# Macaron block (feed-forward, S4 convolution, feed-forward) on one core: first tile reordered, shared low-rank product of A's upper half, PdT copied ahead

## The reference

```
x = x + 0.5 * ffn(layernorm(x))
x = x + s4(layernorm(x))            # causal convolution with a kernel K of length 512, plus D * u
x = x + 0.5 * ffn(layernorm(x))

def qlinear(x, q, scale, A, B):     # 4-bit weights and a low-rank part of rank 32
    w = (q - 7.5) * (scale * 0.005)[:, None]
    return x @ w.T + 0.02 * (x @ A @ B)
def ffn(x):
    h = silu(qlinear(x, gate)) * qlinear(x, up)     # 512 -> 1376
    return qlinear(h, down)                         # 1376 -> 512
```

## Time and profile before

| | |
|---|---|
| median of 3 runs | 589.48 us |
| profiled execution, whole | 588.72 us |
| its span | 586.7 us |
| PE busy | 566.7 us, 97% of the span |
| PE weight loads | 436.4 us, 74% |
| DVE busy | 403.0 us, 69% |
| ACT busy | 303.2 us, 52% |
| POOL busy | 229.5 us, 39% |
| mean granted PE clock | 0.993 of full |

### The profile page before, as it was taken

How to read it: one execution, slowest core, us unless ns; L and a number is a source line. 1 busy time by engine, 2 the same in 40 slices (tenths; PEclk the granted TensorE clock), 3 DMA queues, 4 the chain that set the end, 5 groups by cost and what they waited for, 6 DMA issues and landing times.

```text
span 586.7 us, 12166 instructions
## 1 busy us (share of the span) xinstructions
PE 566.7 (97%) x4656; PEld 436.4 (74%) x4656; DVE 403.0 (69%) x766; ACT 303.2 (52%) x748; POOL 229.5 (39%) x248
## 2 busy tenths in 40 slices
PE   6799998999989999999999999999999999999996
PEld 6544675436678887888778887788877888788975
DVE  6577864886489867599576995479844888455544
ACT  5476412666238851478505784158831676236621
POOL 5446500030205980059701596026850367105510
PEclk9899998999999999999999999999999999999999
DMA  8983302003323074001820019000190202540001
GB/s 287 374 272 120 72 11 69 13 0 64 73 15 14 12 112 86 10 1 20 146 44 10 2 20 177 13 11 1 26 178 11 77 1 43 94 149 5 1 2 73
DMA packets 87266, 39.75 MB, mean 68 GB/s; under 512 B 75849, under 2 KB 80713, under 8 KB 87209
## 3 DMA queue, kind: packets, MB, share of 16 engines
q1 hardware_dynamic: 86393, 38.84, 29.5%
q10 hardware_dynamic: 816, 0.14, 0.1%
HBM read 16.42 MB, written 4.19 MB: 35 GB/s over the span
## 4 chain that ended last, share of the span: by engine, by line
PE 91%; DVE 4%; ACT 2%; issue 1%; DVEq 1%; DMA 1%; ACTq 0%
PE banks L1436 35%; PE banks L1359 28%; PE banks L1419 11%; PE banks L1401 5%; PE banks L1565 4%; PE banks L1324 3%; PE banks L1378 2%; PE banks L1395 1%; ACT p_stack L638 1%; DVEq L858 1%; DMA X<-in_x 1%; PE banks L1554 1%; DVE stats L857 1%; PE banks L1585 0%; DVE zs L869 0%
## 5 line engine op out<-in xcount | busy, mean ns | idle before, releaser
L1436 PE MATMUL banks<-xT,w 128*128 128x256 f16 (+1 forms) x1848 | 223.1, 273 | 1.3 <-DVE ring L996 1.3
L1436 PEld LDWEIGHTS banks<-xT,w 128*128 128x128 f16 (+1 forms) x1848 | 182.0, 100 | 22.7 <-issue 1.8
L1359 PE MATMUL banks<-dw,hT 128*128 128x256 f16 (+3 forms) x1408 | 184.8, 286 | 0.0
L1359 PEld LDWEIGHTS banks<-dw,hT 128*128 128x128 f16 (+1 forms) x1408 | 135.7, 98 | 35.0 <-issue 0.9
L955 DVE SCALAR_TENSOR_TENSOR work<-banks,work 128x512 f32<-128x512 f32 (+1 forms) x88 | 60.6, 689 | 59.3 <-PE banks L1401 25.5
L483 POOL TENSOR_TENSOR rstd<-veps,minus_half 128x1 f32<-128x1 f32 x32 | 19.9, 623 | 182.3 <-DVE veps L861 182.1
L1419 PE MATMUL banks<-xT,w 128*128 128x512 f16 (+1 forms) x336 | 80.0, 382 | 1.6 <-DVE work L955 0.7
L554 POOL TENSOR_TENSOR hT<-work,hT 128x512 f16<-128x512 f32 x60 | 70.8, 1181 | 5.0
L551 POOL TENSOR_SCALAR hT<-work 128x512 f16<-128x512 f32 x60 | 37.8, 630 | 89.1 <-DVE work L955 89.1
L1419 PEld LDWEIGHTS banks<-xT,w 128*128 128x128 f16 (+1 forms) x336 | 33.4, 101 | 42.3 <-ACT work L687 2.6
L638 ACT ACTIVATE p_stack<-banks 128x64 f16<-128x64 f32 x96 | 14.6, 226 | 88.2 <-PE banks L1324 83.5
(11 more groups left out here) (176 smaller groups left out, 704.0 us busy)
## 6 DMA issues: line engine op xcount, KB each, us to landing
out_x<-X SPq DMA_DIRECT2D x16, 256.0 KB, 2.6
X<-in_x SPq DMA_DIRECT2D x1, 2048.0 KB, 8.5
ring<-in_gate_q_t SPq DMA_DIRECT2D x2, 768.0 KB, 12.4
hT<-in_up_q_t SPq DMA_DIRECT2D x2, 768.0 KB, 13.1
work<-in_b SPq DMA_DIRECT2D x2, 688.0 KB, 8.8
X<-in_x SPq DMA_DIRECT2D x4, 256.0 KB, 5.1
X<-in_x SPq DMA_DIRECT2D x1, 1024.0 KB, 13.3
ring<-in_down_q_t SPq DMA_DIRECT2D x1, 1024.0 KB, 11.7
```

The lines of the kernel that those rows point to most:

```text
L1359: last = mm(acc(j)[:, 1 - c, 0:width], hT[0:rows[m], m, a, j * P:(j + 1) * P], dw[0:rows[m], m, src], start=(m == 0 and a == 0), stop=(m = ...
L1436: last = mm(dst[0:r, 0:HH], w[:, blocks + k, cols], xT[:, a, 2 * op + k, :], start=(first and k == 0 and a == 0), stop=(k == 1 and a == 1) ...
```

## The change

It has four parts.

1. The first tile is reordered. `warm` is 96 and 28 products instead of 60 and 12. `p_product(0, 1)` and `first_products` are placed earlier; the transposes of P for sub-tiles 1 to 3 later; block 1 of the up product is made between them. ACT makes the high parts of sub-tiles 2 and 3 instead of DVE; DVE copies the transposed sub-tile 1 instead of ACT. The B matrices arrive in two parts of 256 and 1120 columns (the second after chunk 1); ACT scales the first, POOL the second, after its cast of chunk 1. In DVE's blocks of tile 0, `ln_stats(1, .)`, `down_b` and `ln_apply(1, .)` move to later blocks, `down_a` to block 9, with the weight sums behind it in blocks 9 and 10. The Vc-B product moves from the passes into block 9, into bank 4. `s4_b_copy` and `s4_vectors` stand right behind `s4_inverse`, and PE waits for `s4_b_copy` in front of `down_pass(0, 1, 0, EARLY)` instead of in front of tile 1.
2. In fast tiles `p_product` for i = 0 and 2 makes B11 with A's upper half into columns 0-127 of its bank and B21 with the lower half beside it. For i = 1 and 3 it makes T1 and B22 only (8 instructions instead of 12). DVE copies the B11 part out once for each pair and adds it to each half's own part (`p_sum`) into a buffer in SBUF, from which `p_high` and `p_split` now read.
3. ACT's `pd_copy` of j = 1 and 3 stands in front of `p_high` of the same number.
4. `p_high` of fast tiles waits for `p_sum` instead of for `p_product`.

The diff, cut to the core:

```diff
-        b_raw = view(work, 0, P, 2, I)
+        b_raw = X[:, 2 * TS:SUBS, :].rearrange("p s h -> p (s h)")[:, 0:2 * I].rearrange("p (g i) -> p g i", g=2)
+        b_parts = (slice(0, B_FIRST), slice(B_FIRST, I))
...
             cast_gate(0)
+            cast_gate(1)
             for g, wb in enumerate((gb_w, ub_w)):
...
+                if n < FAST:
+                    act.wait_ge(f.p_mm, n * TS + i + 1)
+                else:
+                    act.wait_ge(f.p_sum, (n - FAST) * TS + i + 1)
...
+                pd_copy(n, 1)
                 if more:
                     p_high(n + 1, 1)
-                pd_copy(n, 1)
...
                 pd_high(n, 3)
+                pd_copy(n, 3)
                 if more:
                     p_high(n + 1, 3)
-                pd_copy(n, 3)
...
+            def p_sum(n, i):
+                dve.wait_ge(f.p_mm, n * TS + i + 1)
+                after(dve, f.p_hi, n * TS + i)
+                own = slice(4 * R * (1 + i % 2), 4 * R * (2 + i % 2))
+                if i % 2 == 0:
+                    V.tensor_copy(p_b11, p_bank(n, i)[:, 0:4 * R]).then_inc(f.p_b11, 1)
+                    dve.wait_ge(f.p_b11, ((n - FAST) * TS + i) // 2 + 1)
+                V.tensor_tensor(p32, p_bank(n, i)[:, own], p_b11, ALU.add).then_inc(f.p_sum, 1)
...
-                        if m in (0, 1):
-                            ln_stats(1, 2 * m, 2 * m + 1)
-                        if m == 2:
+                        if m in (2, 3):
+                            ln_stats(1, 2 * m - 4, 2 * m - 3)
+                        if m == 4:
                             down_b()
-                        if m == 4:
+                        if m in (5, 6, 7, 8):
+                            ln_apply(1, m - 5)
+                        if m == 9:
                             down_a()
-                        if m in (3, 5, 6, 7):
-                            ln_apply(1, (3, 5, 6, 7).index(m))
-                        if m in (8, 9):
-                            weight_sum(m - 8, 0, 1)
+                            weight_sum(0, 0, 1)
+                        if m == 10:
+                            weight_sum(1, 0, 1)
...
                 if n == 0:
                     s4_inverse()
+                    s4_b_copy()
+                    s4_vectors()
...
+                elif i % 2 == 0:
+                    sums(0, half(B11, 0))
+                    last = sums(1, half(B21, 2))
                 else:
+                    last = sums(2, half(T1, 0) + half(B22, 2))
...
                 down_pass(n, 0, 1, EARLY)
+                if n == 0:
+                    pe.wait_ge(s_bread, 1)
                 down_pass(n, 1, 0, EARLY)
...
-            warm(60)
+            warm(96)
             x_transpose(0, 0, 2)
-            warm(12)
+            warm(28)
             x_transpose(1, 1, 3)
             pe.wait_ge(s_aw, 1)
             p_product(0, 0)
+            p_product(0, 1)
             first_products(0)
             x_transpose(2, 2, 2)
-            p_product(0, 1)
+            first_products(1)
             x_transpose(3, 3, 3)
-            first_products(1)
...
```

More of the change, by code:

```diff
@@ L30 @@
 CHUNKS = [(0, 2), (2, 5), (5, 8), (8, 11)]
+B_FIRST = 2 * P
 def s4_macaron(nc, x_d, state_d, step_d, gq_d, uq_d, dq_d, scales_d, ds_d, a_d, b_d, da_d, db_d,
@@ L223, in s4_macaron @@
         s_lr = sem("low_rank_a_loaded")
-        s_lrb = [sem(f"low_rank_b_{g}_loaded") for g in ("gate", "up")]
+        s_lrb = [[sem(f"low_rank_b_{g}_part{c}_loaded") for g in ("gate", "up")] for c in range(2)]
         s_lrd = sem("low_rank_down_loaded")
@@ L568, in _ @@
             cast_gate(0)
+            cast_gate(1)
             for g, wb in enumerate((gb_w, ub_w)):
-                pool.wait_ge(s_lrb[g], 16)
-                pool.tensor_scalar(wb[:, :], b_raw[:, g, :], B_SCALE, 0.0, ALU.mult, ALU.add).then_inc(s_bhi[g], 1)
-            for c in range(1, len(CHUNKS)):
+                pool.wait_ge(s_lrb[1][g], 16)
+                pool.tensor_scalar(wb[:, b_parts[1]], b_raw[:, g, b_parts[1]], B_SCALE, 0.0, ALU.mult, ALU.add)\
+                    .then_inc(s_bhi[g], 1)
+            for c in range(2, len(CHUNKS)):
                 cast_gate(c)
@@ L737, in plain_blocks @@
                         h_high(n, m - 1)
-                    if n == 0 and m in (0, 2, 4):
+                    if n == 0 and m == 0:
+                        p_out(2)
+                        p_out(3)
+                    if n == 0 and m in (2, 4):
                         cast_up(1 + m // 2)
@@ L1068, in tile @@
                     s4_inverse()
+                    s4_b_copy()
+                    s4_vectors()
+                fast = more and n + 1 >= FAST
                 pd_split(n, 0)
@@ L1071, in tile @@
                 pd_split(n, 1)
+                if fast:
+                    p_sum(n + 1, 0)
                 if more:
@@ L1075, in tile @@
                 down_add(n, 0)
-                if n == 0:
-                    s4_b_copy()
+                if fast:
+                    p_sum(n + 1, 1)
                 if more:
@@ L1092, in tile @@
                     conv_add(c * TS + 2)
+                if fast:
+                    p_sum(n + 1, 2)
                 if more:
@@ L1097, in tile @@
                     conv_add(c * TS + 3)
-                if n == 0:
-                    s4_vectors()
                 if s4:
                     s4_row_split()
+                if fast:
+                    p_sum(n + 1, 3)
                 if more:
@@ L1315, in p_product, with sums, half @@
                     pe.wait_ge(f.p_stack, i - 2 if n == 0 else n * TS + i)
+                def sums(out, terms):
+                    for t, (x, c) in enumerate(terms):
+                        last = mm(p_bank(n, i)[:, out * 4 * R:(out + 1) * 4 * R], x, a_w[:, c, :], start=(t == 0),
+                                  stop=(t == len(terms) - 1))
+                    return last
+                def half(op, c):
+                    return [(xT[:, a, 2 * op + k, s % 2 * P:(s % 2 + 1) * P], c + k) for k in range(2) for a in range(2)]
                 if n < FAST:
-                    terms = [(xT_plain[:, a, c, s * P:(s + 1) * P], c) for c in range(KH) for a in range(2)]
-                else:
-                    j = s % 2
-                    ops = ((B11, 0), (B21, 2)) if s < 2 else ((T1, 0), (B11, 0), (B22, 2))
-                    terms = [(xT[:, a, 2 * op + k, j * P:(j + 1) * P], c + k)
-                             for op, c in ops for k in range(2) for a in range(2)]
-                for t, (x, c) in enumerate(terms):
-                    last = mm(p_bank(n, i)[:, 0:4 * R], x, a_w[:, c, :], start=(t == 0), stop=(t == len(terms) - 1))
+                    last = sums(0, [(xT_plain[:, a, c, s * P:(s + 1) * P], c) for c in range(KH) for a in range(2)])
+                elif i % 2 == 0:
+                    sums(0, half(B11, 0))
+                    last = sums(1, half(B21, 2))
+                else:
+                    last = sums(2, half(T1, 0) + half(B22, 2))
                 last.then_inc(f.p_mm, 1)
@@ L1423, in plain_blocks @@
             def plain_blocks(n):
-                for m in range(M):
+                if n == 0:
+                    product(n, 0, 1)
+                    p_transpose(3)
+                    product(n, 1, 1)
                     for g in range(2):
-                        if n or m:
-                            product(n, g, m)
+                        low_rank(n, g, 0)
+                for m in range(0 if n else 2, M):
+                    for g in range(2):
+                        product(n, g, m)
                         if m:
                             low_rank(n, g, m - 1)
+                    if n == 0 and m == M - 2:
+                        state_b()
             def part(m, dst, blocks, op, first, ks=(0, 1)):
@@ L1498, in tile @@
                 down_pass(n, 1, 1, LATE)
-                if n == 0:
-                    pe.wait_ge(s_kin, 128)
-                    for v in range(2):
-                        last = mm(bank[0][:, v:v + 1], vct[:, v, :], bp, start=True, stop=True)
-                    last.then_inc(s_bmm, 1)
                 down_low(n, 0)
@@ L1535, in tile, with state_b @@
                 down_low(n, 3)
+            def state_b():
+                pe.wait_ge(s_kin, 128)
+                for v in range(2):
+                    last = mm(bank[4][:, v:v + 1], vct[:, v, :], bp, start=True, stop=True)
+                last.then_inc(s_bmm, 1)
             def cauchy():
```

70 lines of the change are left out of this document (39 added, 31 removed).

## The result

The changed kernel takes 590.39 us (median of 14 runs, 589.30 to 591.36 us). The kernel before, measured 14 times by now, takes 587.05 us (586.0 to 589.5). The ratio on record is 1.005, 95% interval 1.0038 to 1.0062 (the two medians stand as 1.0057 to 1): the change makes the kernel slower, by a small amount that is clear of noise. The forecast was 588.4 us and no change. The profiled execution took 591.22 us with a span of 589.4 us, 2.7 us longer than the span of before. One execution of the kernel before, among those measured beside experiments 9 to 11, took 1193.75 us; it is in no median and no ratio here.

What follows compares the result with a forecast made beforehand. PE, busy 97%, was taken to bound the kernel. From 588.72 us, -5.3 + 5.9 - 3.6 + 1.9 + 1.55 + 1.8 - 2.1 = +0.15, less 0.3 to 0.5, gave 588.4 us; range 584.0 to 592.5.

Steps and rivals of the forecast that it cites:

- The start: Program start up to PE's third gate/up block: reached at 25.0 us instead of 30.34, -5.3 us.
- End of tile 0: Last blocks of tile 0: new PE waits for down_a (2.3 us) and s4_b_copy (3.4 us), +5.9 us with the small product.
- POOL's norms end at 66.54 us of real time: End of tile 0: POOL's norms keep their old end time, 71.8 us in the old trace's frame, beside DVE's chain.
- The clock at this wait: Behind the 3.4 us wait at the end of tile 0: half-clock running, +1.9 us, bounds 0 to 3.4.
- What it buys: Later passes of tile 0: cauchy wait 1.63 us and half-clock stretch 1.7 us go, pd_copy brings 0.3; -3.6 us.
- the small gain of 0.4: Tile 0's fourth row: a small gain, taking 0.3 to 0.5 us off the sum.
- Tile 1 to tile 2: DVE's longer chain (copy, adds, trip over ACT) delays dsum, for which PE waits: +1.55 us, bounds 0.7 to 2.2.
- The clock behind it: Behind the wait of some 3 us for dsum before tile 2: a half-clock stretch, +1.8 us, bounds 0 to 3.4.
- Fast tile changes: Five changes from tiles 2 to 3 up to 6 to 7: 0.4 to 0.5 us saved each, -2.1 us together.
- DVE blocked by POOL: Rival, end of tile 0: six DVE instructions take 0.7 us more each beside POOL's norms; 592.5 us, chance 0.12.
- Cheap waits: Rival: no clock loss behind new waits, or in one place only; down_a and sums undisturbed; 584.7 us, chance 0.25.
- the start brings little: Rival, program start: PE's order no longer fits its inputs and ACT's chain is 2 to 3 us late; 591 us, chance 0.08.

Runs made afterwards that it cites:

- experiments 9 to 11: Changed kernel, s4_b_copy and down_a early, s4_vectors late: 582.55 us; with row split late, p_sum from tile 3: 579.06; or with 52 identity products before tile 2: 580.51.
- Experiment 12: Only the changed kernel's first tile, with s4_b_copy and down_a early and s4_vectors late; p products and PdT as before: 580.52 us, ratio to before 0.9897.
- experiment 1: Changed kernel with p_product, p_high and p_split of all fast tiles as before (no p_sum): 588.90 us, ratio to before 1.0023.
- experiment 5: Changed kernel with the convolution's kernel-row split moved behind the fourth row's work at the end of tile 1: 589.13 us, ratio to before 1.0029.
- Experiment 3: Changed kernel with down_a in DVE's block 4 of tile 0 instead of block 9: 589.95 us, ratio to before 1.0043.
- experiment 7: The kernel before, unchanged, profiled a second time: 587.05 us.
- Experiment 4: Changed kernel with 52 identity-matrix products in front of tile 2's first product, where PE waits for dsum: 588.29 us, ratio to before 1.0016.
- 2: Changed kernel with s4_b_copy in DVE's block 9 of tile 0 instead of behind s4_inverse: 585.79 us, ratio to before 0.998.
- 8: Changed kernel with s4_b_copy in block 9 and down_a in block 4 of tile 0: 586.41 us, ratio to before 0.999.
- 9: Changed kernel with s4_b_copy in block 9, down_a in block 4, s4_vectors behind tile 0's second down_add, third weight sum at tile 0's end: 582.55 us.
- experiment 6: The kernel before with only pd_copy of j = 1 and 3 put in front of p_high: 588.71 us in one execution.

## Why the prediction was wrong

Place by place the mechanisms came as forecast, and each term lay inside its own bounds but one (what the loss buys, -4.1 us, bounded at -3.6). Several losses were sized too small, and the reference was not typical. Against the profiled execution the forecast gave -0.3 us; it was 2.7 us.

- **The start: right.** -5.37 us against -5.3. Experiment 12 shows that the first tile, with three groups of instructions placed otherwise, is worth 5.9 us on its own.
- **End of tile 0: the first failed step.** Forecast +5.9 us; PE came from -5.37 to +1.88, that is +7.25. The step "POOL's norms end at 66.54 us of real time" took POOL's time from the old profile and so left no wait for them. But POOL loses to DVE as DVE loses to POOL: they ended at 70.42, and `s4_inverse`, which DVE could have begun at 69.83, waited 0.62 us. `h_low` took 1.10 us instead of 0.7, and the Vc-B product 0.53 us (56.39 to 56.92) instead of 0.3. The wait for `down_a` was 2.0 us (2.3 forecast), that for the copy 4.3 (3.4). The same code gave +6.4 us in the profile of experiment 1, with no wait for POOL, and +7.8 us in that of experiment 5, where the inverse waited 1.31 us. So the place of the copy in DVE's order makes most of the wait, as forecast, and POOL adds 0 to 1.3 us. Experiment 3 shows that a shorter chain on DVE does not help then: the wait for POOL grew to 1.88 us.
- **The clock at this wait: right in size,** one stretch of 3.41 us, 1.7 us.
- **What it buys: -4.1 us against -3.6 and the small gain of 0.4.** From +1.88 + 1.7 PE came to -0.52. The parts are 1.63 us in front of `cauchy`, 1.7 us of clock, 0.27 us in the second row and 0.53 us that the Vc-B product no longer takes in the passes. The forecast counted that product as a loss above and not as a gain here, though it says that it only moves; the gap that it expected in the fourth row was not there before. And the 1.7 us are a stretch that the kernel before has in some executions only (experiment 7): in the medians that gain is smaller.
- **Tile 1 to tile 2: +1.84 us against +1.55.** `p_high` takes 0.55 us from SBUF, 0.46 from the bank; the chain is as described.
- **The clock behind it: the second failed step.** Forecast 1.8 us for one stretch. It was 6.83 us at 0.50, and tile 2 takes 2.9 us more than later tiles (73.96 against 71.02 us). Experiment 4 shows that it comes from PE's idle time. The size varies: with the same waits tile 2 took 73.6 to 73.8 us in the profiles of 2, 8 and 9 and 72.38 us in that of 3.
- **Fast tile changes: the third.** -0.31 us each against 0.42. The gap in front of `down_low` went, as forecast, but turned into 0.56 us of waiting for the fourth `p_stack`, and experiment 6 shows that PdT ahead by itself gains next to nothing.
- **The reference.** The three runs of before had a median of 589.48 us, the 14 runs one of 587.05. The profiled execution, from which the sum starts, took 588.72 us, 1.67 us above the latter. A small slip beside it: of the two waits in the earlier trace rows only the first recurs, the second stands once, in front of tile 2.

The range, 8.5 us wide, held the time. What failed is the sign: the misses at the end of tile 0 (+1.3), at the clock (+1.1), at the fast tiles (+0.5) and in the chain (+0.3) have one sign; together they are the miss of 3.0 us in the profiles and 0.2 us that the other terms gave back. Between the medians the kernel lost 3.34 us where -0.3 was forecast: 2.0 us of this miss are how far 590.39 lies above 588.4, and 1.67 us are the reference. That the time came within 2.0 us of the forecast is in part luck: taken from the median of 14 runs, the same sum gives 586.7 us.

Of the rivals, "DVE blocked by POOL" had the place and the pair of engines, and mostly the wrong direction: POOL was held up more (2.23 and 2.60 us) than DVE (0.4 us in `h_low`). "Cheap waits" and "the start brings little" did not happen.

## What to carry to other kernels

An early start is worth only what the engines behind it can follow: after moving a stage earlier, look for instructions that wait for something that did not move, and for what stands behind them in their engine's order. A short copy on which PE waits must not stand behind a long or waiting instruction; here its place was worth 4.6 us. Another engine's end time is no constant of the old profile either: POOL's norms ended anywhere from 67.86 to 70.8 us by the same code in four executions. Price an idle stretch of TensorE with its clock, and take the reference from many runs or several profiles before summing terms of 1 to 2 us.

## What the runs showed of the hardware

- Beside DVE's weight sums POOL's 256-column operations L531 and L528 took 2.60 and 2.23 us, while the sums took 1.65 us a pair; in the profile of before the sums took 2.46 us and the same two operations 1.24 and 1.42. In the profile of experiment 4, where DVE stood idle beside it, L531 took 0.61 us. Which engine loses is not fixed. The Trainium skill (SBUF — State Buffer, "Who interferes with whom") says that whoever issues first holds the shared port; the traces agree in that either side can be the one that waits. They don't show the order: L531 starts at 66.69 us, 0.48 us before the sums that it lost to. Spans on POOL are rough, so this is no proof against the rule.
- A wait of 1.63 us at the same place was followed by 3.41 us at 1.2 GHz in one execution of the kernel before and by none in another. One of 2.98 us, in the profile of experiment 4, was followed by none.
- ACT reads 64 float32 columns in 0.245 us from SBUF (mean of 72, changed kernel) and in 0.226 us from PSUM (mean of 96, kernel before); three in a row take 0.55 against 0.46 us.
